# A state-space layer: B and C projected on 48 rows with the step inputs, then spread to all partitions by two products with a table

## The reference, cut to what matters

```
x_dbl = einsum('bld,ed->ble', u_c, W_x)            # 48 values for each position
dt_r, Bm, Cm = split(x_dbl, [16, 32])
dt = softplus(einsum('blr,dr->bld', dt_r, W_dt) + b_dt)
def step(h, inp):
    dt_t, u_t, B_t, C_t = inp
    h = exp(dt_t[..., None] * A) * h + (dt_t * u_t)[..., None] * B_t[:, None, :]
    return h, einsum('bds,bs->bd', h, C_t)
```

## Time and profile before

| | us |
|---|---|
| median of 3 runs | 3097.12 (3096.05 to 3098.53) |
| profiled execution, its own time | 3085.19 |
| its span, first to last instruction | 3083.4 |
| TensorE busy | 2722.6 (88%) |
| VectorE busy | 1632.8 (53%) |
| ScalarE busy | 1436.1 (47%) |
| GpSimd busy | 1409.5 (46%) |
| mean granted TensorE clock | 0.944 of full speed |

### The profile page before, as it was taken

The page is one execution under the profiler, slowest core; times in us unless marked ns, Lnnn a source line. Parts: engine busy times, 40 slices in busy tenths (PEclk is TensorE's granted clock), DMA queues, the critical chain, the costliest instruction groups (busy, mean ns, idle before and its releaser), DMA issues.

```text
span 3083.4 us, 70976 instructions
## 1 busy us (share of the span) xinstructions
PE 2722.6 (88%) x25057; PEld 2121.9 (69%) x25057; DVE 1632.8 (53%) x3568; ACT 1436.1 (47%) x4586; POOL 1409.5 (46%) x1644
## 2 busy tenths in 40 slices
PE   6888888559989979979995889999996997999999
PEld 6777776436756656655664767877874665768888
DVE  4999999564446655561115763333333224555643
ACT  4666665344456657743336862223231334772310
POOL 3777777442356665543335661323232223663320
PEclk8999999779999999979997999999996998999999
DMA  2000000210000000051112020000007111010100
GB/s 83 3 2 3 3 3 2 64 36 1 24 12 17 15 23 1 12 180 42 45 43 78 0 94 8 11 10 7 10 18 252 32 33 54 1 48 29 53 10 20
DMA packets 75147, 106.19 MB, mean 34 GB/s; under 512 B 11024, under 2 KB 54672, under 8 KB 74656
## 3 DMA queue, kind: packets, MB, share of 16 engines
q1 hardware_dynamic: 68960, 86.68, 8.4%
q0 software_dynamic: 5952, 16.26, 1.7%
HBM read 88.50 MB, written 14.42 MB: 33 GB/s over the span
## 4 chain that ended last, share of the span: by engine, by line
PE 54%; POOL 4%; DVE 4%; ACT 3%; issue 3%; SPq 1%; DMA 1%; DVEq 0%; ACTq 0%; POOLq 0%
PE up_ps L2490 5%; PE e_out_ps L2508 5%; PE t_ps L664 4%; PE s_ps L650 3%; PE bank_a L1554 3%; PE bank_b L1554 3%; POOL probs L569 2%; PE up_ps L2484 2%; ACT probs L798 2%; PE bank_a L612 2%; PE bank_d L701 2%; PE frame_ps L1633 2%; PE bank_b L1570 2%; PE bank_d L620 2%; PE bank_a L1570 2%
## 5 line engine op out<-in xcount | busy, mean ns | idle before, releaser
L569 POOL TENSOR_TENSOR probs<-probs,inv 128x512 f32<-128x512 f32 x320 | 328.0, 1039 | 269.0 <-DVE inv L919 268.6
L3410 POOL TENSOR_TENSOR hc<-h,bc 128x1024 f32<-128x1024 f32 x128 | 302.0, 2359 | 115.3 <-DVE h L3682 90.6
L798 ACT ACTIVATE probs<-s_ps,negmax 128x128 f32<-128x128 f32 (+1 forms) x768 | 297.1, 414 | 5.8 <-DVE negmax L879 4.4
L3682 DVE TENSOR_TENSOR_SCAN h<-da,dbu_ps 128x1024 f32<-128x1024 f32 x128 | 292.5, 2285 | 11.4 <-DVE dbu_ps L3694 4.8
L664 PE MATMUL t_ps<-ident,probs 128*128 128x128 f32 x1280 | 207.7, 285 | 58.7 <-POOL probs L569 50.2
L664 PEld LDWEIGHTS t_ps<-ident,probs 128*128 128x128 f32 x1280 | 138.9, 141 | 125.5 <-POOL probs L569 60.3
L3499 PE MATMUL dta_ps<-dt,a_spread 32*128 32x128 f32 x2048 | 157.6, 294 | 64.8 <-ACT da L3629 39.2
L3629 ACT ACTIVATE da<-dta_ps 128x1016 f32<-128x1016 f32 x128 | 130.2, 1017 | 150.0 <-PE dta_ps L3499 149.6
L3499 PEld LDWEIGHTS dta_ps<-dt,a_spread 32*128 32x128 f32 x2048 | 132.2, 195 | 87.5 <-ACT da L3629 39.0
L2414 POOL DMA_INDIRECT expert_rows_out<-y,row_to x62 | 61.1, 986 | 268.8 <-DVE y L2773 138.3
L879 DVE TENSOR_REDUCE negmax<-s_ps 128x4 f32<-128x1024 f32 (+1 forms) x128 | 156.6, 1223 | 45.1 <-PE s_ps L650 43.4
(11 more groups left out here) (511 smaller groups left out, 6750.6 us busy)
## 6 DMA issues: line engine op xcount, KB each, us to landing
cT<-in_ctx_turned SPq DMA_DIRECT2D x32, 256.0 KB, 2.6
w_down<-in_L_ffn_w SPq DMA_DIRECT2D x8, 1024.0 KB, 11.8
w_up<-in_L_ffn_w SPq DMA_DIRECT2D x8, 1024.0 KB, 13.0
c_in<-in_ctx SPq DMA_DIRECT2D x16, 256.0 KB, 3.0
w_gate<-in_L_ffn_w SPq DMA_DIRECT2D x8, 512.0 KB, 6.6
w_up<-in_L_ffn_w SPq DMA_DIRECT2D x8, 512.0 KB, 8.4
w_down<-in_L_ffn_w SPq DMA_DIRECT2D x8, 512.0 KB, 8.6
w_gate<-expert_rows_out SPq DMA_DIRECT2D x8, 512.0 KB, 6.4
```

What stands on the lines that cost most here:

```text
L569: pool.tensor_tensor(probs[:, u % 2, i], probs[:, u % 2, i], inv[:, u % 2, HB * i:HB * (i + 1)].unsqueeze(2).broadcast_to([P, HB, W]), ALU ...
L798: last = act.activation(probs[:, u % 2, i, k, :], src, ACT.Exp, bias=negmax[:, u % 2, at], accum_out=sums[:, u % 2, at])
L3410: pool.tensor_tensor(hc[:, s % 4], h[:, s % 2], bc[:, j, 1, :].unsqueeze(1).broadcast_to([P, 2 * G, P]), ALU.mult).then_inc(hc_ready.sem, 1)
L3682: dve.tensor_tensor_scan(flat(h[:, s % 2]), flat(da[:, s % 4]), dbu_ps[s % 2][:, :, :, :].rearrange("p i g t -> p (i g t)"), 0.0, ALU.mult ...
```

## The change

`project_xd` multiplies uc by all 48 columns of W_x in four products and leaves the result on 48 partitions of `front`, part 0. `copy_xd` copies these 48 rows into `xd`, and `step_sizes` uses the first 16. A new table `which_state` (48 x 2 x 128, ones where row 16 + 16 * what + n meets the eight partitions of state n) comes from the host by one more DMA. A new TensorE step `spread_bc` multiplies it with `xd`, one product for B and one for C, into parts 2 and 3 of `front`; ScalarE's new `copy_bc` copies them into `bc`. `w_bc` and its two copies on VectorE are gone. The users of `bc` wait for the new semaphore `bc_ready` in place of `xd_ready`, and the next writers of `front` (`project_u`, `out`) for `bc_ready` as well.

```diff
-    a_spread, w_bc = sb("a_spread", [P, IC, G, P]), sb("w_bc", [P, IC, 2, P])
+    a_spread, which_sb = sb("a_spread", [P, IC, G, P]), sb("which_state", [XD, 2, P])
...
+                 (which_sb[:, :, :], which_state[:, :, :]),
                  (w_out_sb[:, :, :], chunked(w_out)))
...
             def weigh_states(b, j, s):
                 if s == 0:
-                    pool.wait_ge(xd_ready.sem, xd_ready.done(b))
+                    pool.wait_ge(bc_ready.sem, bc_ready.done(b))
...
             def project_u(b, j):
+                pe.wait_ge(bc_ready.sem, bc_ready.done(b - 1))
...
             def project_xd(b, j):
                 for m in range(IC):
-                    pe.matmul(front[0:R, 0, :], w_x_sb[:, m, 0:R], uc[:, j, m, :], start=(m == 0), stop=(m == IC - 1))
+                    last = pe.matmul(front[0:XD, 0, :], w_x_sb[:, m, :], uc[:, j, m, :], start=(m == 0), stop=(m == IC - 1))
+                last.then_inc(xd_made.sem, 1)
+
+            def spread_bc(b):
+                pe.wait_ge(pre_ready.sem, pre_ready.done(b))
                 for what in range(2):
-                    for m in range(IC):
-                        last = pe.matmul(front[:, 1 + what, :], w_bc[:, m, what, :], uc[:, j, m, :],
-                                         start=(m == 0), stop=(m == IC - 1))
-                last.then_inc(xd_made.sem, 1)
+                    last = pe.matmul(front[:, 2 + what, :], which_sb[:, what, :], xd[:, :], start=True, stop=True)
+                last.then_inc(bc_made.sem, 1)
...
             def out(b, j, after):
                 pe.wait_ge(pre_ready.sem, pre_ready.done(after))
+                pe.wait_ge(bc_ready.sem, bc_ready.done(after))
...
             def unit(b, j, first, left):
                 for s in range(H):
                     spread_out(half_at(b, j, s + 2, left), half_at(b, j, s + 1, left))
+                    if s == 3 and left:
+                        spread_bc(b + 1)
...
-            pe.wait_ge(prep.sem, prep.done(2))
+            pe.wait_ge(prep.sem, prep.done(1))
             project_xd(0, 0)
             convolve(1, y_ps, 0)
             convolve(1, y_ps, 1)
             step_sizes(0, 0)
+            spread_bc(0)
...
             def copy_xd(b, j):
                 act.wait_ge(xd_made.sem, xd_made.done(b))
                 act.wait_ge(dt_made.sem, dt_made.done(b - 1))
+                act.wait_ge(bc_made.sem, bc_made.done(b - 1))
+                act.activation(xd[:, :], front[0:XD, 0, :], ACT.Copy).then_inc(xd_ready.sem, 1)
+
+            def copy_bc(b, j):
+                act.wait_ge(bc_made.sem, bc_made.done(b))
                 act.wait_ge(hc_ready.sem, hc_ready.done(H * (b - 2) + H - 1))
-                act.activation(xd[:, :], front[0:R, 0, :], ACT.Copy)
-                act.activation(bc[:, j], front[:, 1:3, :], ACT.Copy).then_inc(xd_ready.sem, 1)
+                act.activation(bc[:, j], front[:, 2:4, :], ACT.Copy).then_inc(bc_ready.sem, 1)
...
                     if s == 3 and left:
                         take_steps(b + 1, 1 - j)
+                        copy_bc(b + 1, 1 - j)
...
-            for what in range(2):
-                last = dve.tensor_copy(w_bc[:, :, what, :].rearrange("p m (n e) -> p m n e", e=PER),
```

More of the change, by code:

```diff
@@ L3315, in depool_ternary_stage, with mamba_stage @@
         return Stage(sync, gpsimd, tensor, scalar, vector, y2_ready, Later(x_saved))
-def mamba_stage(core, x, x_turned, spread, gather, w_in, conv_w, conv_b, w_x, w_dt, b_dt, a_log, d_skip, w_out, after=None):
+def mamba_stage(core, x, x_turned, spread, gather, which_state, w_in, conv_w, conv_b, w_x, w_dt, b_dt, a_log, d_skip, w_out, after=None):
     nc, loads = core.nc, core.weight_loads()
@@ L3335, in mamba_stage @@
         spread_sb, gather_sb = sb("spread", [P, G, P]), sb("gather", [P, G, ROWS])
-        a_spread, w_bc = sb("a_spread", [P, IC, G, P]), sb("w_bc", [P, IC, 2, P])
+        a_spread, which_sb = sb("a_spread", [P, IC, G, P]), sb("which_state", [XD, 2, P])
         taps, skip = sb("taps", [P, IC, K, P]), sb("skip", [P, IC, P])
         u, z_raw = sb("u", [P, IC, K - 1 + P]), sb("z_raw", [P, 2, IC, P])
-        uc, sz, xd, bc = sb("uc", [P, 2, IC, P]), sb("sz", [P, 2, IC, P]), sb("xd", [R, P]), sb("bc", [P, 2, 2, P])
+        uc, sz, xd, bc = sb("uc", [P, 2, IC, P]), sb("sz", [P, 2, IC, P]), sb("xd", [XD, P]), sb("bc", [P, 2, 2, P])
         pre, low, high = sb("dt_pre", [P, IC, P]), sb("dt_low", [P, IC, P]), sb("dt_high", [P, IC, P])
@@ L3360, in mamba_stage @@
         y_summed, passed = c("y_summed"), c("waits_passed")
+        bc_made, bc_ready = c("squared"), c("squared_x")
         consts, prep, prep_a = c("constants_made"), c("prep_done"), c("prep_a")
@@ L3480, in step_sizes @@
                 for m in range(IC):
-                    last = pe.matmul(front[:, m, :], w_dt_sb[:, m * P:(m + 1) * P], xd[:, :], start=True, stop=True)
+                    last = pe.matmul(front[:, m, :], w_dt_sb[:, m * P:(m + 1) * P], xd[0:R, :], start=True, stop=True)
                 last.then_inc(dt_made.sem, 1)
@@ L3664, in scalar @@
             soften_log(0, 0)
+            copy_bc(0, 0)
             decay((0, 0, 0))
@@ L3691, in weigh_inputs @@
                 if s == 0:
-                    dve.wait_ge(xd_ready.sem, xd_ready.done(b))
+                    dve.wait_ge(bc_ready.sem, bc_ready.done(b))
                 spread_in = halves(dbu_ps[s % 2][:, :, :, :])
@@ L3724, in vector @@
             last.then_inc(prep.sem, 1)
-            for what in range(2):
-                last = dve.tensor_copy(w_bc[:, :, what, :].rearrange("p m (n e) -> p m n e", e=PER),
-                                       w_x_sb[:, :, R + N * what:R + N * (what + 1)].unsqueeze(3).broadcast_to(
-                                           [P, IC, N, PER]))
-            last.then_inc(prep.sem, 1)
             for m in range(IC):
@@ L3751, in mamba_stage @@
         consts.advance(1)
-        prep.advance(3)
+        prep.advance(2)
         prep_a.advance(1)
+        for n in (bc_made, bc_ready):
+            n.advance(B)
         return Stage(sync, gpsimd, tensor, scalar, vector)
@@ L3788, in build @@
         rows_out = nc.dram_tensor("expert_rows_out", ((2 * B + tiles_of(2)) * P, D), F32).ap()
-        run(core, setup, mamba_stage(core, a["x"], a["x_turned"], a["spread"], a["gather"], a["L0_attn_W_in"], a["L0_attn_conv_w"],
+        run(core, setup, mamba_stage(core, a["x"], a["x_turned"], a["spread"], a["gather"], a["which_state"], a["L0_attn_W_in"], a["L0_attn_conv_w"],
                               a["L0_attn_conv_b"], a["L0_attn_W_x"], a["L0_attn_W_dt"], a["L0_attn_b_dt"],
@@ L3855, in state_rows @@
     gather = (at[None, None, :32] == 8 * np.arange(4)[None, :, None] + at[:, None, None] % 8)
-    return spread.astype(np.float32), gather.astype(np.float32)
+    row, what = np.arange(48)[:, None, None], np.arange(2)[None, :, None]
+    which = (row == 16 + 16 * what + at[None, None, :] // 8)
+    return spread.astype(np.float32), gather.astype(np.float32), which.astype(np.float32)
 def wide_head_rows():
@@ L3891, in laid_out @@
     a["ctx_turned"] = a["ctx_2048"].reshape(B, P, CC, P).transpose(0, 3, 2, 1)
-    a["spread"], a["gather"] = state_rows()
+    a["spread"], a["gather"], a["which_state"] = state_rows()
     a["head_rows"] = wide_head_rows()
```

## The result

The change makes the kernel slower: 3124.94 us (median of 7 runs, 3114.62 to 3136.27) against 3097.12 us (7 runs, 3093.75 to 3098.95), ratio 1.0091, 95% interval 1.007 to 1.0113. The forecast was 3105.4 us with a range up to 3114.

A forecast was written before the change was run, and what follows sets the result against it. VectorE was taken to set the pace in the state-space stage, with TensorE's order of work deciding its waits. +1.3 us without the clock plus +7.0 for clock falls gave +8.3 on 3097.1, so 3105.4 us; range 3093 to 3114.

The forecast's parts named there:

- What bounds the kernel: State-space stage: VectorE, busy 28.76 of 30.43 us a unit, sets the pace; only shortening its waits can shorten the stage.
- the ring: Theory drawn up after the result: closed TensorE-ScalarE chain from project_xd through decays of states 5, 6, 2 back sets unit length.
- The chain through the projection: VectorE's wait for the output projection, behind spread_bc's two products: 0.50 - 0.12 = +0.38 us in an even unit.
- The moved copy and its wait: copy_bc ahead of state 5's decay on ScalarE: +0.64 us, costing 0.26 us behind five branches, hidden behind other units.
- the sum without the clock: All terms of start and units together, before any falls of TensorE's clock: +1.3 us.
- The removed products: project_xd loses eight wide products, 1.98 us; only 0.12 us are had, 1.24 after a fall; a gap of some 1.9 remains.
- The start: project_xd(0) loses its wide products, so the first weighting comes earlier: -2.0 us.
- The clock: Thin stretch ahead of step 2's spread lowers TensorE's clock in two of five of eleven units: 4.4 falls, +7.0 us.
- Rival C: The clock falls in nearly each of the eleven units: +18.9 us, 3116.0 us; chance 0.12.

The follow-up runs named there:

- late_copy: Changed kernel with copy_bc moved behind the decay of state 5 on ScalarE instead of ahead of it; 3118.9 us, ratio 1.0057.
- fill: Changed kernel with seven products that nobody reads put ahead of the four of project_xd; 3116.77 us, ratio 1.0057.
- few_wide: Kernel before with two wide products for B and C in place of eight, nothing else new; 3098.61 us, ratio 0.9997.
- unrolled_after: Changed kernel with the state-space stage's loop of six unit pairs written out; 3132.21 us, ratio 1.011.
- unrolled_before: Kernel before with the state-space stage's loop of six unit pairs written out; 3077.37 us, ratio 0.9931.
- swap_late: Changed kernel with copy_bc behind the decay of state 5 and, at step 1, project_xd ahead of the sum over states; 3106.11 us, ratio 1.0023.
- fill_late: Changed kernel with seven unread products ahead of project_xd and copy_bc behind the decay of state 5; 3108.2 us, ratio 1.0027.

## Why the prediction was wrong

- **What bounds the kernel.** This step failed. VectorE is busy 28.77 of 30.43 us, but in the changed kernel the unit's length is set by the ring; VectorE's wait for the projection is where the ring's slack shows, not the path. late_copy shows it: with the projection's place in TensorE's order kept, moving one copy gave 0.69 us a unit. The chain through the projection, which the prediction priced, is close by: with spread_bc in it, it comes to 0.12 us more than an even unit of before, once the copy is off the ring.
- **The moved copy and its wait.** Its size was near (0.64 us forecast; the rows give 8.04 - 7.23 = 0.81, with spread_bc at 0.64 us for the forecast 0.50). That it is hidden behind units without a branch, since VectorE waits for no spread there, was wrong: the lateness travels on to the next project_xd. It costs 0.81 us in each of some 14 units, an estimate of 11.3 us from the even units, where the sum without the clock had +3.3 us for all units (+1.3 with the start).
- **The removed products.** As forecast: of 1.98 us 0.11 were had, the rest became a gap of 1.77 us (forecast 1.9), and the 0.9 us wait at step 2 behind a fall is gone. The wait right behind a branch grew by 0.44 and 0.50 us in units 5 and 7 (forecast 0.26).
- **The start.** First scan 1.3 us earlier in the first pair of profiles and 2.5 in the second (forecast 2.0). From the start of project_xd(0) on it is 1.8 us in both (22.12 us before, 20.35 and 20.36 after); the rest is when that product started, which varied from profile to profile.
- **The clock.** The mechanism was right and was shown (fill, few_wide, unrolled_after), the term too small: 4.4 falls of 1.6 us, 7.0 us, were forecast. In the two profiles after, what the units grew by beyond the ring's 11.3 us is 18.5 - 11.3 = 7 us and 33.3 - 11.3 = 22 us (sums of the unit windows 490.77 and 509.38 against 472.32 and 476.13), 14.6 us on the mean. The mis-sized part is the price. The forecast took it from three falls behind branches, in which the clock was low for about 4 us. In the changed kernel it was low for about 7 us behind four branches of the first profile and for 10 to 14 us in five even units of the two, which took 35.85 to 37.59 us instead of 31.1 to 31.2; only unit 10 of the first profile came near the forecast price (32.78 us). Rival C, with +18.9 us, was the nearest case. With the start and the ring in place of its 1.3 us it would come to -2.0 + 11.3 + 17.6 = +26.9 us, near the measured 26 to 28, but by luck: its eleven falls of 1.6 us are not what the profiles show.
- **Shorter gaps.** With an idle gap of 1.77 us the clock fell in 12 of 13 units of unrolled_after, while in unrolled_before, where wide products fill that gap, it fell in none. The Trainium skill, page "TensorE: Matmul & The Clock Gate", section "Why this matters for your kernels", warns only of longer gaps. The measurements decide against reading shorter ones as safe.

On the means of the two profiles of each kernel the stage grew by 24.0 us: -1.9 for the start, 11.3 for the ring, 14.6 for the clock. The forecast was right on the start and some 8 us short on each of the other two.

What stays open: the last 7 to 10 us between swap_late or fill_late and the kernel before. About 2 us are in units without a fall, each 0.1 us or more longer; the rest goes with falls of the clock, whose cause in the swapped order wasn't isolated.

## What to carry to other kernels

Where engines hand work round in a ring, idle time on the busiest engine is the ring's slack, so cost a new wait by the length of the closed chain that it lies in, in every round. Taking work off TensorE ahead of a wait for another engine buys nothing if that engine was nearly as late, and can cost TensorE's clock for the dense work behind it; fill such a gap with work that is needed anyway, or leave it filled, and look whether the move has opened a thin stretch elsewhere. Before trimming products, look for what makes the clock fall already: here writing out the loop gave the kernel before 21 us, and the changed kernel, with its gap in every unit, nothing.

## What the hardware showed that was not expected

- Work added without use made the kernel faster: seven products more in each unit, 3124.8 to 3116.8 us, and with the late copy 3118.9 to 3108.2 us.
- After a gap of 1.77 us the granted clock stayed at its lower level for 6.6 us in which TensorE was busy all the time (windows above), and in that unit for some 14 us in all.
- At the five loop branches TensorE stood for 1.65 to 2.16 us without instructions (two profiles of before), and falls of the clock came with them: without branches 13 units in a row kept the full clock, and the kernel before took 3077.37 instead of 3098.65 us.
- The later stages, with unchanged code, took 2533.3 us in the first profile of before and 2538.1 to 2551.2 us in the seventeen others; spans of single profiles can't be compared more finely than that.
